# Four GNN layers on one core: each indirect gather gets the table's last row as a bound on its indices

## The reference

```python
aggr = segment_sum(x[src], dst)                                   # layer 0
h = elu((x + aggr) @ W1 + b1); x = layernorm(x + h @ W2 + b2)

msg = relu(concat(x[src], x[dst], edge_attr) @ mW1 + mb1) @ mW2 + mb2   # layer 1
x = layernorm(x + mlp(concat(x, segment_sum(msg, dst))))

h = relu(batchnorm(l2norm(mean_{dst}(x[src]) @ Wl1 + b1 + x @ Wr1)))    # layer 2, first half
out = l2norm(mean_{dst}(h[src]) @ Wl2 + b2 + h @ Wr2)                   # layer 2, second half
x = layernorm(x + l2norm(out + x))

msg = x[src] @ weight[edge_type]                                  # layer 3
x = layernorm(x + segment_sum(msg, dst))
```

## Time and profile before

| what | value |
|---|---|
| time, median of 3 runs | 9608.49 us (9607.45 to 9609.73) |
| the profiled execution, from its first to its last instruction | 9611.7 us |
| GpSimd busy | 7166.3 us, 75% |
| TensorE busy (matmul) | 4955.0 us, 52% |
| VectorE busy | 2604.7 us, 27% |
| ScalarE busy | 1301.8 us, 14% |
| software DMA queue of the gathers | 242,880 packets, 349.17 MB, 16.2% of 16 engines |
| chain that ended last | GpSimd 70%, "issue" 23%, TensorE 3% |

### The profile page before, as it was taken

The page is one execution under the profiler, slowest core; times in us unless marked ns, Lnnn a source line. Parts: engine busy times, 40 slices in busy tenths (PEclk is TensorE's granted clock), DMA queues, the critical chain, the costliest instruction groups (busy, mean ns, idle before and its releaser), DMA issues.

```text
span 9611.7 us, 127811 instructions
## 1 busy us (share of the span) xinstructions
PE 4955.0 (52%) x23790; PEld 4259.7 (44%) x23791; DVE 2604.7 (27%) x6055; ACT 1301.8 (14%) x2785; POOL 7166.3 (75%) x7594
## 2 busy tenths in 40 slices
PE   4555555566666666344444445666666633333333
PEld 3444444456666665333333334555555522222222
DVE  2222222234444444111121223333333311111111
ACT  1111111111111111000000002222222200000000
POOL 7777777777777777777777777777777667777777
PEclk7555555577777777555555555555555555555555
DMA  3111111133333333111111112222232211111111
GB/s 76 34 34 34 35 34 35 34 93 96 95 94 96 95 95 92 29 31 32 31 32 32 31 31 72 82 83 81 80 84 80 76 32 30 30 30 30 30 30 29
DMA packets 460729, 529.13 MB, mean 55 GB/s; under 512 B 220578, under 2 KB 287616, under 8 KB 459848
## 3 DMA queue, kind: packets, MB, share of 16 engines
q0 software_dynamic: 242880, 349.17, 16.2%
q1 hardware_dynamic: 93785, 88.18, 3.3%
q10 hardware_dynamic: 123247, 83.52, 3.0%
HBM read 442.93 MB, written 77.29 MB: 54 GB/s over the span
## 4 chain that ended last, share of the span: by engine, by line
POOL 70%; issue 23%; PE 3%; ACTq 2%; ACT 1%; DVE 1%; SPq 0%; DMA 0%; POOLq 0%; DVEq 0%
POOL G L520 70%; PE PH L1282 1%; PE PAG L1282 1%; ACTq L383 1%; ACTq L391 1%; PE NA L1282 0%; SPq L422 0%; ACT G L755 0%; PE NB L1282 0%; DVE G L1153 0%; ACT STG L680 0%; ACT Y L663 0%; ACT XT L590 0%; DMA rel_tab<-STG 0%; DVE Y L1038 0%
## 5 line engine op out<-in xcount | busy, mean ns | idle before, releaser
L1282 PE MATMUL PAG<-OH,G 128*64 128x96 f32 (+2 forms) x12126 | 2294.9, 382 | 3742.0 <-DMA G<-rel_tab,IDX 988.0
L1282 PEld LDWEIGHTS PAG<-OH,G 128*64 128x64 f32 (+2 forms) x12126 | 2097.5, 253 | 3971.2 <-issue 3425.2
L520 POOL DMA_INDIRECT G<-rel_tab,IDX x1507 | 1421.9, 944 | 515.7 <-issue 459.6
L520 POOL DMA_INDIRECT G<-far_tab,SRC x1527 | 1440.8, 944 | 485.3 <-issue 465.5
L520 POOL DMA_INDIRECT G<-h_tab,SRC x1524 | 1439.4, 944 | 480.7 <-issue 463.5
L520 POOL DMA_INDIRECT G<-in_x,SRC x1525 | 1440.6, 945 | 475.2 <-issue 464.6
L520 POOL DMA_INDIRECT G<-x_tab,SRC x1507 | 1423.4, 945 | 477.1 <-issue 459.7
L941 DVE TENSOR_TENSOR AGG<-AGG,PAG 64x96 f32 (+2 forms) x980 | 245.8, 251 | 5434.9 <-PE PAG L1282 5432.6
L905 DVE TENSOR_TENSOR OH<-CONST,DREL 128x768 f32<-128x768 f32 x980 | 926.9, 946 | 3.2 <-issue 2.3
L1282 PE MATMUL PAG<-OH,HT 128*128 128x96 f32 x3126 | 615.7, 378 | 583.2 <-ACT HT L748 579.0
L1282 PEld LDWEIGHTS PAG<-OH,HT 128*128 128x128 f32 x3126 | 572.8, 283 | 630.3 <-ACT HT L748 625.3
(11 more groups left out here) (173 smaller groups left out, 3896.4 us busy)
## 6 DMA issues: line engine op xcount, KB each, us to landing
GROWS<-x_tab SPq DMA_DIRECT2D x4096, 0.2 KB
GROWS<-rel_tab SPq DMA_DIRECT2D x4096, 0.2 KB
GROWS<-in_x SPq DMA_DIRECT2D x3584, 0.2 KB
GROWS<-h_tab SPq DMA_DIRECT2D x3456, 0.5 KB
rel_tab<-STG ACTq DMA_DIRECT2D x200, 250.0 KB
GROWS<-far_tab SPq DMA_DIRECT2D x3072, 0.5 KB
GROWS<-x_tab ACTq DMA_DIRECT2D x3072, 0.2 KB
GROWS<-rel_tab ACTq DMA_DIRECT2D x3072, 0.2 KB
```

What stands on the lines that cost most here:

```text
L520: pool.indirect_dma_start(out=G[:, h, j, 0:tabs[p].shape[1]], out_offset=None, in_=tabs[p], in_offset=bass.IndirectOffsetOnAxis(ap=numbers ...
L1282: return nc.tensor.matmul(dst, lhsT, rhs, start=start, stop=stop, skip_group_check=True)
```

## The change

Each indirect gather of `gathers` is given a bound on its indices, the number of its table's last row, and is told that an index beyond it is skipped and is no error. Before, no bound was given.

```diff
                     pool.indirect_dma_start(
                         out=G[:, h, j, 0:tabs[p].shape[1]], out_offset=None, in_=tabs[p],
                         in_offset=bass.IndirectOffsetOnAxis(ap=numbers[:, c:c + 1], axis=0),
+                        bounds_check=tabs[p].shape[0] - 1, oob_is_err=False,
                     ).then_inc(gathered[h], 16 * (GROUP - j if j == filled - 1 else 1))
```

## The result

The changed kernel takes 9998.14 us (median of 4 runs, 9996.01 to 9999.5) against 9608.43 us of the kernel before (4 runs, 9607.45 to 9609.73): a ratio of 1.0405, with a 95% interval of 1.039 to 1.042. It is 389.7 us slower, 51.3 ns for each of the 7,590 gathers. The forecast was 10,060 us.

A forecast was written before the change was run, and what follows sets the result against it. GpSimd was taken to bound the kernel, with gathers one after the other. Profiled span 9611.7 + 448 (check) + 3 (moved waits) = 10,063 us, so 10,060 us for the median; range 9,600 to 11,000 us.

The forecast's parts named there:

- The bound of the kernel: GpSimd's own time makes the span: 7,590 gather periods of 1,249 ns, 944 busy plus 305 issue gap, one after the other.
- the waits between passes: Waits for other engines' work on the last units of a pass; claimed to stay at 108 us.
- The indices: None is beyond its table, so nothing is skipped and rows, packets and bytes stay the same; cost and gain 0.
- The register moves: 7,590 moves on GpSimd's sequencer, one ahead of each gather; claimed covered by the running gather, cost 0.
- the bare move: Rival: moves between gathers are not covered, 61 ns each, 463 us, and the check is free; 10,075 us, chance 8%.
- The moved waits: Waits now sit on the register move ahead of a gather; about 0.49 us at no more than 10 places, 3 us taken.
- The check: Inside each gather, comparing 128 indices with the bound, for all partitions at once; 59 ns each, 448 us; case's chance 45%.
- one of the prediction's own signs: The whole forecast would be wrong if a gather's time grew with something other than the number of indices.
- the upper bound of 7.4 ns for an index: Most that a check made index by index inside a gather could cost: 944 / 128 ns each, 944 ns a gather.
- the index-by-index rival: Rival: the gather checks each index separately, say 236 ns a gather, 11,400 us; over 120 ns, chance 12%.
- Nothing added: Rival: the gather's program compares anyway or ignores the bound, under 2.5 ns added, moves covered; 9,612 us, chance 30%.
- Faster: Rival: the bounded gather takes a shorter path; with 20 ns less per gather 9,457 us, chance 5%.

## Why the prediction was right

**The bound of the kernel.** Right. The span was written down as 7,590 periods of GpSimd with nothing over them, and 52 ns more in each came out in full: 397.3 us of busy time, 383.8 us of span. The 14 us between them were given back by the waits, chiefly the one for `rel_tab`, 8.9 us shorter. That small term was not in the sum: I had let the waits between passes stay.

**The indices: 0.** Right; 242,880 packets and 349.17 MB, as before.

**The register moves: 0, covered.** Right, and shown from one side: taken away they bring nothing (1.0408 for 1.0405, gaps of 305 ns with and without). Moves without a bound were never measured, since the kernel meant for it has none in its trace. The reading of the one place in the trace where the sequencer worked under a gather carried this; the 463 us of the bare move would have doubled the loss. But it understated the cover: the sequencer is not one gather ahead but 12, and needs 0.54 us for a move and a gather where a period is 1.3 us.

**The moved waits: 3 us.** Right in its mechanism and in the price of one: 0.52 us for a wait against the 0.49 taken. The sum is not shown: the 3.1 us of idle time between the kernels with and without moves fit it, but two builds of the same work differ by 2.4 us. The waits that are over in time are read 12 gathers earlier, not one as the prediction has it, and still cost nothing that shows: GpSimd's rows of waits together went from 121.3 to 122.3 us.

**The check: 59 ns, 448 us.** The right term, sized a little high: 52 ns by the profile, 51.3 ns by the medians, 390 us. A price that hardly falls with fewer indices fits the case taken, all indices at once, but does not show that a comparison is what is paid. It does clash with one of the prediction's own signs, that the whole would be wrong if a gather grew with something other than the number of indices: the term taken was itself a fixed one, so that sign was badly chosen. The row of a GpSimd instruction of 98 to 118 ns was a good measure for an upper bound, but taking half of it was a choice, and its closeness is partly luck. A wrong step stands beside it, though it didn't enter the sum: the upper bound of 7.4 ns for an index, 944 / 128. It took all of a gather for work on its indices. The runs with fewer indices show 0.87 ns for an index on average and, as an estimate, some 830 ns fixed, so the index-by-index rival had its upper end about eight times too high, and 11,000 us as the end of the range was wider than rows could have justified had this been known. The trace before had no gather of another size, so it could not show that.

**The rivals.** Nothing added: refuted, the gather grew by 52 ns. The bare move: refuted by the kernel with the register set once and by gaps of 305 ns. Index by index: refuted by the gathers of 64, 32 and 16 indices. Faster: refuted. What in the code the fixed 40 ns are (reading the register, another path through the program, a comparison made for all indices at once) stays open; the runs only say that they are paid once for each gather, and that with an error in place of skipping a gather of 128 indices takes 13 ns more.

## What to carry to other kernels

When one engine's period times its count gives the span, price a change by what it adds to that period, and ask of each part whether it runs in the engine or in the sequencer ahead of it: here 29 ns of register move cost nothing, under a sequencer that runs 12 gathers ahead, and 52 ns inside the gather cost 4%. When an instruction is added to see what it costs, count it in the trace: one whose result nobody reads may not be in the built program. A bound on indices that are known to be valid is worth leaving out, and if it must be there, skipping is cheaper than an error. Since a gather's cost hardly falls with fewer indices, fill each with all 128.

## What was not expected

- A gather is nearly all fixed cost: 847 ns for 16 indices and 944 ns for 128, with about 305 ns of gap behind either. The Trainium skill calls descriptor generation small in DMA: Bandwidth & Descriptors, Anatomy of one DMA, and says that many descriptors can be emitted before they show in the time. The second half agrees with 0.87 ns for an index; the first doesn't, for in this kernel a gather's 944 ns are what bounds the time.
- Treating an index beyond the bound as an error costs more than skipping it, 1,010 against 997 ns.
- The queue's packets count gathers, not rows: 32 for each gather, whether it has 128 indices or 16, none skipped or nearly all, while the bytes fall from 349.17 to 4.51 MB.
- GpSimd's sequencer is 12 gathers ahead of the one that starts: 773 moves for 761 gathers after 1,000 us.
- A wait on a register move ahead of a gather delays the gather by 0.78 us after its release, a wait on the gather itself by 0.26 us.
